# The block in front of a selective scan: input in four parts, one normalisation pipeline for both images, positions added tile by tile

## The chip, the cores and the metric

The kernel runs on one core of a Trainium2 chip. A core has TensorE (PE; PEld is its weight load), VectorE (DVE), ScalarE (ACT), GpSimd (POOL) and SyncE (SP), which here issues the DMAs. The metric is the time of one execution on the device in microseconds; a time "before" or "after" is the median of several.

## The reference

A chain of layers on two images of 256 channels and 48x48 pixels (2304 tokens): a bidirectional selective scan, linear attention, softmax attention, a graph mixture, sigmoid attention and a mixture of experts. Only the very first steps matter here:

```
x:   (2, 256, 2304)                          # channels x tokens, for each image
m, v = mean(x, channels), mean((x - m)**2, channels)
xn   = (x - m) * rsqrt(v + 1e-5) * ln_g + ln_b
xn  += pos_scale * pos                       # pos: (256, 2304), the same for both images
xz   = xn @ in_proj_w.T                      # then convolution, projections, the scan
```

Beside the input the scan needs weights in SBUF, among them the diagonal matrices `ddiag` (the D of each direction on a diagonal), the negated convolution bias `ncb` and `-exp(A_log)` in `alog`.

## The kernel before

Channels lie on the 128 partitions in two halves (`KC` = 2), tokens along the free dimension. `k.X` holds both images, 128 x 2 x 4608 f32. A tile is `T` = 384 tokens, so an image has `NT` = 6 tiles. A block (`nc.Block()`) holds one instruction stream for each engine; all engines meet at its end. `fresh` is a small block after it in which SyncE clears the semaphores that the block used.

The order in front of the scan is written out by hand, block by block:

- `build` sets `k.eps5` in a block (L3796) and calls `load_constants` (L68): SyncE issues the two images (L76) and three 128x128 constants (L80), identity, mean weights and group weights, and waits for all of them.
- `mamba_input` (L247), first block: SyncE issues `pos`, `gb` (gain and bias of the normalisation) and `pscale` on the semaphore `pos_in` (L258 to L260), and ten weight DMAs on `params` (L262 to L270). It waits for none of them, but the block ends when SyncE has issued them.
- `norm_image` (L86), once for each image, a software pipeline over six tiles with three buffers. For one tile: POOL adds the two channel halves (L110); TensorE multiplies by the mean weights (L124), which gives the mean on all partitions in PSUM; DVE subtracts it (L150); ACT squares (L171); POOL adds the halves of the squares (L114); TensorE sums over channels into three columns (L132); ACT takes the root (L178), DVE the reciprocal (L155); TensorE spreads the three columns over all partitions with the identity as moving operand (L139); DVE multiplies (L162). In its stream each engine takes the later steps of earlier tiles behind the first step of a new one, and waits for semaphores in that order.
- `mamba_input`, last block: ACT scales `pos` by `pscale` and adds the bias (L279, two instructions of 2304 columns), then makes `ncb` and `alog` (L282 to L285); DVE multiplies X by the gain and adds `pos` (L295, four of 2304 columns); POOL makes the eight diagonals (L303); SyncE stores the padding (L309).
- `mamba_chunks`: the scan, 20 chunks of 64 steps; its first instruction that reads X is the matmul of L501. Its per-step work: ACT L796, POOL L934, DVE L978 and L989, TensorE L624.

## Time and profile before

| | us |
|---|---|
| median of 3 runs | 5541.01 (5525.89 to 5549.51) |
| the profiled execution | 5545.61 |
| its span, first to last instruction | 5543.8 |
| first matmul of the scan | 97.5 |
| mean granted clock of TensorE | 0.948 of full |

Busy over the span: PE 4723.3 us (85%), DVE 3434.4 (62%), POOL 2317.8 (42%), ACT 2126.5 (38%). The page's 40 slices are 139 us each, so all that the change touches lies in the first of them. There the page can't resolve anything; the views used are the timeline, the waits, the groups of instructions and the table of stretches, all restricted to the first 100 us, and a few rows from later stages that show an operation or a collision that the first 100 us don't have. In the timeline a row is: start in us, time in us, engine, line, operation, written and read tensors, shapes, count (instructions of a kind that follow each other are merged, and the time is that of all of them), and in brackets the engine's idle time before it with what ended it.

### The profile page before, as it was taken

What the parts mean: (1) busy time and instruction counts of PE and PEld (TensorE: products, weight loads), DVE (VectorE), ACT (ScalarE), POOL (GpSimd) and SP (SyncE); (2) the same over time, 40 slices, a digit from 0 to 9 for tenths busy, and PEclk for the clock granted to TensorE, in tenths of its full rate; (3) what the DMA queues carried; (4) which work ended last, traced back from release to release, by engine and by line L of the source; (5) the groups of instructions that cost most, each with busy time, mean ns of one, the idle gap of its engine ahead of it and who ended that gap; (6) DMA issues with size and microseconds to landing.
All of it is one profiled execution on the core that took longest, in us unless ns stands there. A gap on an engine that the chain in (4) does not pass through costs nothing. (4 is left out here: it accounts for less than half of the span.)

```text
span 5543.8 us, 51619 instructions
## 1 busy us (share of the span) xinstructions
PE 4723.3 (85%) x14958; PEld 2624.9 (47%) x14959; DVE 3434.4 (62%) x5148; ACT 2126.5 (38%) x3464; POOL 2317.8 (42%) x2114
## 2 busy tenths in 40 slices
PE   5787788988878888799899899596999899996798
PEld 3333333433323333355455655464555555555576
DVE  2999999999999999679387365264232101003232
ACT  2666666656656666232232222111222222112232
POOL 2888898888889888302111100461000000003111
PEclk7999999999999999999999899798999999995899
DMA  2434443443444443100100001110112000001222
GB/s 85 153 111 145 141 124 123 131 128 117 131 141 130 130 136 109 61 31 6 50 30 15 31 4 42 22 16 15 58 43 89 2 0 2 0 8 36 64 73 93
DMA packets 222219, 391.88 MB, mean 71 GB/s; under 512 B 35986, under 2 KB 205752, under 8 KB 217116
## 3 DMA queue, kind: packets, MB, share of 16 engines
q1 hardware_dynamic: 213852, 383.83, 21.6%
q0 software_dynamic: 8128, 5.27, 0.6%
q8 instruction: 101, 1.65, 0.1%
q14 instruction: 138, 1.13, 0.1%
HBM read 337.13 MB, written 58.23 MB: 71 GB/s over the span
## 5 line engine op out<-in xcount | busy, mean ns | idle before, releaser
L934 POOL TENSOR_TENSOR DBU<-DU,BB 128x461 f32<-128x461 f32 (+1 forms) x1280 | 1372.3, 1087 | 291.7 <-DVE PS L978 279.3
L624 PE MATMUL PS<-G,ident 128*128 128x461 f32 (+1 forms) x2560 | 1138.1, 570 | 385.2 <-DVE G L989 382.5
L978 DVE TENSOR_TENSOR_SCAN PS<-PS,HC,DBU 128x461 f32<-128x461 f32 (+1 forms) x1024 | 1149.5, 1168 | 3.9 <-ACT PS L796 2.5
L796 ACT ACTIVATE PS<-DT,alog 128x461 f32<-128x461 f32 (+1 forms) x1280 | 825.1, 645 | 727.5 <-DVE PS L978 726.7
L624 PEld LDWEIGHTS PS<-G,ident 128*128 128x128 f32 x2560 | 451.9, 190 | 1034.8 <-DVE G L989 822.7
L989 DVE TENSOR_TENSOR G<-PS,CB 128x461 f32<-128x461 f32 (+1 forms) x1280 | 786.6, 625 | 3.4 <-PE PS L624 3.4
L3074 DVE TENSOR_TENSOR X<-X,PS 128x768 f32 x12 | 11.5, 954 | 554.0 <-PE PS L3041 554.0
L3030 PE MATMUL PS<-QT,N 128*128 x864 | 310.1, 486 | 5.5 <-ACTq L3047 5.5
L3041 PE MATMUL PS<-AT,XT 128*128 128x384 f32 x864 | 310.4, 487 | 0.0
L1367 POOL TENSOR_TENSOR X<-X,FF x12 | 42.5, 3542 | 636.7 <-ACT EV L1362 636.7
L978 DVE TENSOR_TENSOR_SCAN PS<-PS,DBU 128x461 f32<-128x461 f32 (+1 forms) x256 | 271.7, 1106 | 57.8 <-POOL DBU L934 55.7
L3105 POOL TENSOR_TENSOR xs<-X 128x384 f32 x12 | 11.7, 989 | 700.6 <-issue 700.6
L1043 PE MATMUL PS<-TT,w_fc 128*128 x768 | 280.9, 494 | 12.2 <-ACTq L1067 12.2
L1053 PE MATMUL PS<-H,w_fc 128*128 128x384 f32 x768 | 275.3, 486 | 0.0
L3063 ACT ACTIVATE AT<-PS 128x384 f32<-128x384 f32 x216 | 105.3, 490 | 416.8 <-PE PS L3030 416.8
L523 PE MATMUL PS<-XI,cdiag 128*128 128x461 f32 (+1 forms) x640 | 260.0, 549 | 0.6 <-ACT XI L680 0.6
L2968 DVE TENSOR_TENSOR Hg<-Hg,GB 128x384 f32<-128x384 f32 x144 | 80.3, 558 | 258.9 <-ACT Hg L2950 248.1
L1081 ACT ACTIVATE H<-PS,b_fc 128x384 f32<-128x384 f32 x192 | 111.0, 580 | 325.7 <-PE PS L1043 325.6
L3030 PEld LDWEIGHTS PS<-QT,N 128*128 128x128 f32 x864 | 164.0, 190 | 119.9 <-issue 5.9
L3041 PEld LDWEIGHTS PS<-AT,XT 128*128 128x128 f32 x864 | 163.7, 190 | 115.5 <-issue 2.6
L2923 PE MATMUL PS<-NN,w1g 128*128 128x384 f32 x576 | 209.4, 492 | 4.4 <-PEq L57 4.4
L2937 PE MATMUL PS<-Hg,w2g 128*128 128x384 f32 x576 | 207.3, 488 | 0.0
(446 smaller groups left out, 7459.0 us busy)
## 6 DMA issues: line engine op xcount, KB each, us to landing
BB<-proj_dram SPq DMA_DIRECT2D x256, 461.0 KB, 4.0
CB<-proj_dram SPq DMA_DIRECT2D x64, 922.0 KB, 6.0
BB<-proj_dram SPq DMA_DIRECT2D x64, 460.0 KB, 4.7
ew<-in_l_w SPq DMA_DIRECT2D x16, 1024.0 KB, 5.7
CB<-proj_dram SPq DMA_DIRECT2D x16, 920.0 KB, 5.9
w_fc<-in_l_w_fc SPq DMA_DIRECT2D x4, 2048.0 KB, 11.7
XI<-xi_dram SPq DMA_DIRECT2D x8, 928.0 KB, 5.0
xi_dram<-XI SPq DMA_DIRECT2D x8, 922.0 KB, 6.5
```

Of the source, the lines that this page charges most:

```text
L523: mm = pe.matmul(PS[:, 2 + j % 2, :wide(h)], w.cdiag[:, j, t, :], XI[:, j, at:at + wide(h)], start=(t == 0), stop=(t == TAP - 1))
L624: pe.matmul(PS[:, j, :wide(g)], k.ident[:], G[:, S % 4, :wide(g)], start=False, stop=(n == DS - 1))\
L796: act.activation(DA(S), DT[:, j, :wide(g)], ACT.Exp, scale=w.alog[:, chunk(g)[1], j, n:n + 1]).then_inc(da_done, 1)
L934: pool.tensor_tensor(DBU[:, S % 4, :wide(g)], DU[:, j, :wide(g)], BB[:, 2 * u + n % 2, :wide(g)], ALU.mult).then_inc(dbu_done, 1)
L978: dve.tensor_tensor_scan(flow(HS(S), g), flow(DA(S), g), flow(DBU[:, S % 4, :wide(g)], g), start, ALU.mult, ALU.add).then_inc(h_done, 1)
L989: dve.tensor_tensor(G[:, S % 4, :wide(g)], HS(S), CB[:, n, :wide(g)], ALU.mult).then_inc(g_done, 1)
L1043: mm = pe.matmul(k.PS[:, s % 3, :T], w1(j, s), src(j, c), start=(j == 0), stop=(j == KC - 1))
L1053: mm = pe.matmul(k.PS[:, 4 + 2 * u + o, :T], w2(m, o), H[:, m, :], start=(m == 0), stop=(m == NM - 1))
L2923: mm = pe.matmul(k.PS[:, s % 3, :T], w1[:, j, s * P:(s + 1) * P], g.NN[:, j, c * T:(c + 1) * T], start=(j == 0), stop=(j == KC - 1))
L2937: mm = pe.matmul(k.PS[:, 4 + 2 * u + o, :T], w2[:, m, o * P:(o + 1) * P], H[:, m, :], start=False, stop=(m == NM - 1))
L3030: mm = pe.matmul(k.PS[:, s % NA, :T], k.N[:, j, s * P:(s + 1) * P], QT[:, j, bass.ds(c * T, T)], start=(j == 0), stop=(j == KC - 1))
L3041: mm = pe.matmul(k.PS[:, 4 + 2 * u + o, :T], XT[:, m, o * P:(o + 1) * P], AT[:, m % NA, :], start=(m == 0), stop=(m == LT - 1))
```

## The change

`load_constants`, `norm_image` and the blocks of `mamba_input` become one block. SyncE issues x in four parts of three tiles, each on its own semaphore, in the order part 0, mean weights, `gb`, `pscale`, part 1, `pos`, part 2, part 3, identity, group weights, then the ten weight DMAs, and then waits for the padding's memset and stores it. All twelve tiles of both images run through one pipeline. The variance is summed by a matmul with the full mean weights, so it stands on all partitions at once (384 columns instead of three, and no spreading matmuls); ACT takes its logarithm, drains, and takes the exponential of -0.5 times that, in place of the root, reciprocal and spread. DVE then multiplies each half of a tile by gain and 1/sigma in one instruction with two SBUF inputs (two instructions of 384 columns), and adds `pos` to the first half; POOL adds `pos` to the second half. ACT scales `pos` in step 3 of the pipeline. The diagonals are made by ACT after the last tile. The block uses 22 semaphores.

```diff
-        load_constants(nc, ctx, k, A)
@@ mamba_input
+    DEEP = 3
+    NV = NB * NT
+    PART = 3
...
+            @block.sync
...
+                load_x(0)
+                sp.dma_start(k.mean_w[:], A["c_mean"]).then_inc(mean_in, 16)
                 sp.dma_start(gb[:], A["l0_ln"]).then_inc(pos_in, 16)
                 sp.dma_start(pscale[:], A["L0_conv_pos_scale"].rearrange("(o n) -> o n", o=1)
                              .broadcast_to([P, 1])).then_inc(pos_in, 16)
+                load_x(1)
+                sp.dma_start(pos[:], A["c_pos"]).then_inc(pos_in, 16)
+                load_x(2)
+                load_x(3)
+                sp.dma_start(k.ident[:], A["c_ident"]).then_inc(const_in, 16)
+                sp.dma_start(k.group_w[:], A["c_group"]).then_inc(const_in, 16)
...
+            @block.gpsimd
...
+                for s in range(NV + 4):
+                    if s < NV:
+                        if s % PART == 0:
+                            pool.wait_ge(x_in[s // PART], 16)
+                        if s >= DEEP:
+                            pool.wait_ge(mean_ready, s - DEEP + 1)
+                        pool.tensor_tensor(xs[:, s % DEEP, :], tile(s)[:, 0, :], tile(s)[:, 1, :], ALU.add)\
+                            .then_inc(x_summed, 1)
+                    if 2 <= s <= NV + 1:
+                        v = s - 2
+                        pool.wait_ge(squared, v + 1)
+                        pool.tensor_tensor(sq[:, v % DEEP, 0, :], sq[:, v % DEEP, 0, :], sq[:, v % DEEP, 1, :], ALU.add)\
+                            .then_inc(sq_summed, 1)
+                    if s >= 4:
+                        v = s - 4
+                        pool.wait_ge(scaled, v + 1)
+                        if v == 0:
+                            pool.wait_ge(pos_done, KC)
+                        n = tile(v)[:, 1, :]
+                        pool.tensor_tensor(n, n, pos[:, 1, v % NT * T:(v % NT + 1) * T], ALU.add)
...
+            @block.tensor
...
+                for s in range(NV + 1):
+                    if s < NV:
+                        pe.wait_ge(x_summed, s + 1)
+                        if s >= DEEP:
+                            pe.wait_ge(centered, s - DEEP + 1)
+                        pe.matmul(k.PS[:, s % DEEP, :T], k.mean_w[:], xs[:, s % DEEP, :], start=True, stop=True)\
+                          .then_inc(mean_ready, 1)
+                    if s >= 1:
+                        v = s - 1
+                        pe.wait_ge(sq_summed, v + 1)
+                        if v >= DEEP:
+                            pe.wait_ge(logged, v - DEEP + 1)
+                        pe.matmul(k.PS[:, DEEP + v % DEEP, :T], k.mean_w[:], sq[:, v % DEEP, 0, :], start=True, stop=True)\
+                          .then_inc(var_ready, 1)
...
             @block.scalar
             def _(act):
+                act.preload_act_table_set("natural_log_exp_and_others")
+                act.wait_ge(eps_set, 1)
+                for s in range(NV + 1):
+                    if s < NV:
+                        act.wait_ge(centered, s + 1)
+                        if s >= DEEP:
+                            act.wait_ge(var_ready, s - DEEP + 1)
+                        act.activation(sq[:, s % DEEP, :, :], tile(s), ACT.Square).then_inc(squared, 1)
+                    if s >= 1:
+                        v = s - 1
+                        act.wait_ge(var_ready, v + 1)
+                        if v >= DEEP:
+                            act.wait_ge(scaled, v - DEEP + 1)
+                        act.activation(rstd[:, v % DEEP, :], k.PS[:, DEEP + v % DEEP, :T], ACT.Ln, bias=k.eps5[:])\
+                           .then_inc(logged, 1)
+                        act.drain()
+                        act.activation(rstd[:, v % DEEP, :], rstd[:, v % DEEP, :], ACT.Exp, scale=-0.5).then_inc(inverted, 1)
+                    if s == 3:
+                        act.wait_ge(pos_in, 48)
+                        for c in range(KC):
+                            act.activation(pos[:, c, :], pos[:, c, :], ACT.Identity, bias=gb[:, c, 1:2], scale=pscale[:])\
+                               .then_inc(pos_done, 1)
                 act.wait_ge(params, 160)
+                act.wait_ge(const_in, 32)
+                for d in range(2):
+                    for j in range(JD):
+                        act.activation(w.ddiag[:, d, j, :], k.ident[:], ACT.Copy, scale=w.vec[:, d, j, 1:2])
...
             @block.vector
             def _(dve):
+                dve.memset(k.eps5[:], 1e-5).then_inc(eps_set, 1)
                 dve.memset(w.neg1[:], -1.0)
...
+                for s in range(NV + 3):
+                    if s < NV:
+                        dve.wait_ge(mean_ready, s + 1)
+                        mean = k.PS[:, s % DEEP, :T].rearrange("p (o t) -> p o t", o=1).broadcast_to([P, KC, T])
+                        dve.tensor_tensor(tile(s), tile(s), mean, ALU.subtract).then_inc(centered, 1)
+                    if 2 <= s <= NV + 1:
+                        v = s - 2
+                        if v == 0:
+                            dve.wait_ge(pos_in, 48)
+                        dve.wait_ge(inverted, v + 1)
+                        for c in range(KC):
+                            n = tile(v)[:, c, :]
+                            op = dve.scalar_tensor_tensor(n, n, gb[:, c, 0:1], rstd[:, v % DEEP, :], ALU.mult, ALU.mult)
+                        op.then_inc(scaled, 1)
+                    if s >= 3:
+                        v = s - 3
+                        if v == 0:
+                            dve.wait_ge(pos_done, KC)
+                        dve.wait_ge(scaled, v + 1)
+                        n = tile(v)[:, 0, :]
+                        dve.tensor_tensor(n, n, pos[:, 0, v % NT * T:(v % NT + 1) * T], ALU.add)
         fresh(nc, used)
```

## Rows read from the trace of the kernel before

**Rows 1.** Table of stretches: start:end, us; busy of PE, PEld, DVE, ACT, POOL; clock; DMA.

```profile
15.30:27.60 12.30, 0.00 (x0) 0.00 (x0) 0.00 (x0) 0.12 (x1) 0.00 (x0) 1.00 0.73 271
52.60:82.10 29.50, 24.15 (x84) 19.33 (x84) 12.52 (x19) 6.20 (x12) 11.67 (x12) 0.51 0.00 1
...
sum 97.50, PE 42.66 PEld 33.13 DVE 35.17 ACT 21.50 POOL 36.97; mean PE 8.53 PEld 6.63 DVE 7.03 ACT 4.30 POOL 7.39
```

**Rows 2.** Waits, 0 to 95 us: who waited for whom, total, times, longest.

```profile
POOL xs L110 <- SPq L102: 32.0, 2, 27.1
```

**Rows 3.** Timeline, the first tiles of image 0.

```profile
27.60 2.88 POOL L110 TENSOR_TENSOR xs<-X 128x384 f32<-128x384 f32 x3 [27.12 <-SPq L102]
...
30.32 0.95 DVE L150 TENSOR_TENSOR X<-X,PS 128x768 f32<-128x768 f32 x1 [29.42 <-PE PS L124]
...
36.25 0.95 DVE L150 TENSOR_TENSOR X<-X,PS 128x768 f32<-128x768 f32 x1 [1.02 <-PE PS L124]
```

**Rows 4.** Timeline, late tiles of image 0.

```profile
43.04 0.94 DVE L150 TENSOR_TENSOR X<-X,PS 128x768 f32<-128x768 f32 x1
...
44.49 0.81 PE L124 MATMUL PS<-xs,mean_w 128*128 128x384 f32 x2
...
45.14 0.92 DVE L162 TENSOR_TENSOR X<-X,PS 128x768 f32<-128x768 f32 x1
45.98 0.95 DVE L150 TENSOR_TENSOR X<-X,PS 128x768 f32<-128x768 f32 x1
```

**Rows 5.** Timeline, TensorE in image 1.

```profile
68.54 1.49 PE L124 MATMUL PS<-xs,mean_w 128*128 128x384 f32 x2
...
72.38 1.49 PE L124 MATMUL PS<-xs,mean_w 128*128 128x384 f32 x2
```

**Rows 6.** Timeline, the last two blocks' borders.

```profile
81.11 0.95 DVE L162 TENSOR_TENSOR X<-X,PS 128x768 f32<-128x768 f32 x1 [0.33 <-PE PS L139]
83.15 0.11 POOL L299 MEMSET pad<- 128x12 f32 x1 [6.34 <-POOLq L57]
...
93.94 2.66 POOL L303 TENSOR_SCALAR ddiag<-ident,vec 128x128 f32<-128x128 f32 x1
97.48 0.11 POOL L876 MEMSET XI<- 128x12 f32 x1 [0.88 <-POOLq L57]
```

**Rows 7.** The line that loads x (L76, issued at 1.17 and 1.7).

```profile
DMA to landing us min/median/max: 8.1/10.6/13.2
```

**Rows 8.** Groups on ScalarE: line, operation, shapes, count; busy us, mean ns; idle.

```profile
L1081 ACT ACTIVATE H<-PS,b_fc 128x384 f32<-128x384 f32 x192 | 111.0, 580 | 325.7 <-PE PS L1043 325.6
...
L279 ACT ACTIVATE pos<-pos,gb,pscale 128x2304 f32<-128x2304 f32 x2 | 4.5, 2299 | 4.6 <-PEq L57 4.6
...
L285 ACT ACTIVATE alog<-alog 128x128 f32<-128x128 f32 x1 | 0.3, 309 | 0.0
```

**Rows 9.** Timeline, diagonals on POOL beside the positions on VectorE.

```profile
84.51 1.18 POOL L303 TENSOR_SCALAR ddiag<-ident,vec 128x128 f32<-128x128 f32 x2
...
85.59 2.62 DVE L295 SCALAR_TENSOR_TENSOR X<-X,gb,pos 128x2304 f32<-128x2304 f32 x1 [2.31 <-ACT pos L279]
85.67 3.01 POOL L303 TENSOR_SCALAR ddiag<-ident,vec 128x128 f32<-128x128 f32 x1
```

**Rows 10.** Timeline, a POOL addition beside VectorE's copies in a later stage.

```profile
2463.39 2.47 POOL L1367 TENSOR_TENSOR X<-X,FF  x1 [154.32 <-ACT EV L1362]
2464.10 6.53 DVE L1832 COPY_PREDICATED V<-MV,V 128x4095 int32<-128x4095 int16 x1
...
2482.26 4.92 DVE L1832 COPY_PREDICATED V<-MV,V 128x4094 int32<-128x4094 int16 x1
...
3054.20 1.80 POOL L1369 TENSOR_TENSOR X<-X,EV 128x768 f32 x1 [0.16 <-issue]
```

**Rows 11.** Table of stretches, the scan and the last stages (columns as in rows 1).

```profile
250.00:355.00 105.00, 83.69 (x200) 35.12 (x200) 105.00 (x161) 64.70 (x97) 89.82 (x85) 1.00 0.43 127
...
4700.00:5543.00 843.00, 744.77 (x2820) 515.28 (x2820) 173.48 (x573) 215.24 (x414) 106.69 (x108) 0.89 0.15 45
```

More of the change, by code:

```diff
@@ L275, in _ @@
             @block.scalar
             def _(act):
-                act.wait_ge(pos_in, 48)
-                for c in range(KC):
-                    act.activation(pos[:, c, :], pos[:, c, :], ACT.Identity, bias=gb[:, c, 1:2], scale=pscale[:])\
-                       .then_inc(pos_done, 1)
+                act.preload_act_table_set("natural_log_exp_and_others")
[20 more added lines that the diff above has]
+                               .then_inc(pos_done, 1)
@@ L3792, in build @@
         k.rd_in = [ctx.enter_context(nc.semaphore(f"rd_in{u}")) for u in range(NU)]
-        with nc.Block() as block:
-            @block.vector
-            def _(dve):
-                dve.memset(k.eps5[:], 1e-5)
-        load_constants(nc, ctx, k, A)
         if start <= 0 <= upto:
```

160 lines of the change are left out of this document (29 added, 131 removed).

## Prediction

> **What bounds the kernel now.** The kernel is a row of stages, one after the other, and the change touches only what lies ahead of the scan. So I first read the table of stretches up to the scan's first matmul, at 97.5 us [rows 1]: loading takes 15.3 us with no engine at work; another 12.3 us pass in which the DMA engines are busy and still no engine; image 0's normalisation takes 25 us, image 1's 29.5 with the gap before it, the positions 15.4. No engine is busy for more than 42.7 of the 97.5 us, so the stretch is bound by its order. The waits [rows 2] name what orders the first part: POOL's additions wait 32.0 us for SyncE's queue, 27.1 of it in one piece. In the code, SyncE issues thirteen DMAs in `mamba_input`'s first block, and every engine waits at the block's end before `norm_image` may start: POOL's first addition comes at 27.60 [rows 3], though x was in by 15.
>
> Then the pace of one tile. In image 0 the chain of subtraction, square, root, reciprocal and product, each engine's step behind another's, closes in 2.94 us (subtractions at 43.04 and 45.98) [rows 4]. In image 1 the granted clock is 0.51, the 1.2 GHz level [rows 1], and TensorE is occupied without a gap: 3.84 us for a tile (68.54 to 72.38) [rows 5]. Between two blocks with the clearing of ten semaphores lie 1.1 us (82.06 to 83.15); from POOL's end to the scan, with six, 0.9 (96.60 to 97.48) [rows 6].
>
> **The change part by part.** The sum is one for the time of the scan's first matmul, now 97.5; what comes after is the same code.
>
> *Start.* x comes in four parts of 1.18 MB. The two images landed 8.1 and 13.2 us after issues at 1.17 and 1.7, at 9.3 and 14.9 [rows 7]; a part is half an image, 2.8 us of that pace, so part 0 lands at 6.5. The mean weights, 64 KB, land some 0.5 us behind it, before POOL's first sum is done (0.96 us [rows 3]). `pos` has part 0, the small ones and part 1 ahead of it: 4.8 MB with itself, as much as was loaded by 15.1, so it lands at about 15.5. Parts 2 and 3 land at 18.5 and 21.5, before POOL needs them; the weights behind them are needed only at the end. Nothing waits any more for SyncE's issuing.
>
> *First three tiles.* The first subtraction came 2.72 us after POOL's first sum and the third 8.65 after [rows 3], which gives 9.2 and 15.2; the fourth, behind a mean that TensorE takes after two variances, at 17.8. The new wait for `pos_in` on VectorE stands before the scaling of tile 0, at 16: `pos` is just in. Behind that wait would be queued all of VectorE's later subtractions.
>
> *The stall.* At step 3 ScalarE, after tile 3's square and tile 2's logarithm and exponential (to 21.0), scales all of `pos`: two activations of 2.30 us [rows 8], to 25.5. Behind them are queued every later square; VectorE's first addition waits for both, and behind that addition the subtraction of tile 4; POOL's first position addition waits too, and behind it the sum of tile 5. So tile 4's subtraction starts, behind tile 0's addition and a POOL addition that holds it off (below), at 26.8, not at 21. Before, the same activations cost 2.31 us of waiting [rows 9].
>
> *Pace of a tile from there.* POOL has three additions of 384 columns. Three of them in a row take 2.88 us [rows 3], so that is the pace by POOL alone. VectorE has the subtraction (0.84 from start to start, 45.14 to 45.98 [rows 4]), two scalings and an addition of 384 columns from SBUF. The trace has no such scaling; the nearest row is the same instruction at 2304 columns, 2.62 us [rows 9], a sixth of which is 0.44; the upper end is the subtraction of 768 from PSUM, 0.84. I take 0.44, the like instruction, and 2.2 us for a tile. ScalarE: square 0.84; a logarithm from PSUM with a bias, 0.58 by the activation of that shape [rows 8]; an exponential, at most the same: 2.0 us, and the drain before the exponential, which no row shows, has 1 us of slack under either pace. TensorE: two matmuls of 384 columns, each 1.49 us at the lower level and 0.81 at the upper [rows 4, 5]: 1.6 to 3.0 us; the short matmuls that made variance and spread go. By busy time alone POOL is the bound, near 2.95.
>
> But VectorE and POOL get into each other's way, and here the trace is plain. POOL's diagonal product, 0.59 us alone (two in 1.18 [rows 9]), took 3.01 when VectorE's scaling with two SBUF inputs had begun 0.08 us before it [rows 9]; the last one took 2.66, ending 0.5 after VectorE's last scaling [rows 6]. The other way round: VectorE's predicated copy of 4095 columns took 6.53 us while a POOL addition of 768 columns was under way, against 4.92 for 4094 columns without one; so it lost 1.61 us to an addition that takes 1.80 alone [rows 10]. In the changed loop VectorE's three new instructions all have two SBUF inputs and POOL is always adding. An addition of 384 columns holds VectorE off for 1.61/2 = 0.80 us; so the shared time of a tile is 3 x 0.80 + 3 x 0.44 = 3.7 us, and 3 x 0.96 + 3 x 0.44 = 4.2 if the whole instruction holds. I take 3.9, between them and nearer the first because that is a measured hold. Ends: 2.95 with no collisions, 4.5 with 0.1 us lost at each of three changes of hand.
> The Trainium skill, "SBUF — State Buffer", section "SBUF: two separate sides", has this as a rule against such a change: a VectorE instruction with two SBUF inputs and a GpSimd instruction lock each other out for the whole instruction. The trace agrees on the lock, but shows 1.61 of 1.80 us held and, in the products, less; by the rule the pace is 4.2 and the sum 2.1 us later, and with no such lock it would be 6.6 us earlier.
>
> *Seven tiles*, from tile 4's to tile 11's subtraction: 7 x 3.9 = 27.3, to 54.1.
>
> *End.* Behind tile 11's subtraction: 0.95, square 0.84, sum 0.96 (and 0.3 waiting), variance 1.7 (a matmul of 1.49 and its end), logarithm and exponential 1.16: 5.9 us. Then ScalarE makes the eight diagonals that POOL made: the nearest rows are its 128-column activations, 0.31 us [rows 8]; 8 x 0.32 = 2.6, and negation, exponential and product for `ncb` and `alog` 0.8. POOL's and VectorE's last additions end about a microsecond earlier. End of ScalarE: 54.1 + 5.9 + 3.4 = 63.4. The block's end and the clearing of semaphores: 1.1 us with ten, 0.9 with six [rows 6], so 0.05 to 0.06 for each, and 0.9 + 16 x 0.06 = 1.85 with 22. The scan starts at 65.2.
>
> *Costs at nothing.* The removed table load of the root lay beside a variance that it had to wait for; the new preload lies in the 6.5 us of loading. The padding's memset and stores go out while tiles are worked on, in front of nothing on SyncE. TensorE idles before the scan in both kernels, so its first matmuls find the clock alike.
>
> *Sum.* 97.5 - 65.2 = 32.3 us less. Against the profiled execution, 5545.6 (span 5543.8 and 1.8 around it): 5513.3. That execution lies 4.6 above the median of 5541.0, and its first 97 us hold no reason for that, so I take the median: 5541.0 - 32.3 = 5508.7.
>
> **Rivals.**
> (a) *No collisions at the pace of the loop.* For it: VectorE's two-input instructions are short and POOL's could fall in between. Against: [rows 9, 10], and POOL would never be idle. Pace 2.95: the end is 7 x 0.95 = 6.6 us earlier; 5502.1.
> (b) *The parts don't come one by one*, or `pos` comes late: part 0 is complete only when parts behind it are, at about 15. Tile 0 then starts 8.7 us later, `pos` is no further wait, and 8.5 us of the gain go; a `pos` landing at 24 instead would cost 6.8. Against: image 0 landed 5.6 us before image 1 though they were issued 0.5 apart [rows 7]. 5541.0 - 23.8 = 5517.2. This is also the case in which the change doesn't do what it says.
> (c) *Slower: the clock in a later stage.* The stretch 4700 to 5543 ran at 0.89 of full clock with TensorE busy 88% of it [rows 11]; the same code took 2.94 us for a tile at the upper and 3.84 at the lower level [rows 4, 5]. If everything after the scan, starting 32 us earlier, meets the clock's changes at other places and this stretch gets 0.82, it is 843 x 0.89/0.82 - 843 = 72 us longer: 5581. It decides from a loss of 60 us on, which is a mean clock of the whole of about 0.937 in place of 0.948. Against: the runs of one kernel would then differ by as much, and they lie within 24 us. The scan itself can't be upset: VectorE is 100% busy in it [rows 11].
> (d) *Part of the gain given back downstream* without a nameable wait, by runs as such: they spread 12 us to either side of the median.
>
> **How the numbers follow.** Main case 0.60, (a) 0.13, (b) 0.18, (c) 0.04, the rest a mixture (0.05). A measurement of this kernel can tell 0.5%, 27.7 us, from no change. The main case lies 4.6 beyond that bound; with its own range, paces 3.5 to 4.5 (2.8 and 4.2 us), and the spread between medians of three, 7 of 10 of it is faster; of (a) 9 of 10, of (b) 3 of 10. That is 0.42 + 0.12 + 0.05 and a little of the rest: 0.60 faster, 0.36 same, 0.04 slower. Range: low is (a) less the run spread, 5502 - 12 = 5490; high is (b) with it, 5517 + 12 = 5529.
>
> **What would show it.** Part 0's first addition at 6.5; a hole between tile 3's and tile 4's subtractions of about 9 us, ended by the activations of `pos`; then subtractions 3.9 us apart, POOL's additions with a mean of 1.2 us or more in place of 0.99, and VectorE's 384-column instructions far above 0.5; ScalarE last, the scan's first matmul at 65. I am wrong if POOL's additions stay at 1.0 us and the pace at 3.0 (a), if POOL starts at 15 (b), if the diagonals or the 22 semaphores take several microseconds, or if the stages behind the scan differ by more than 15 us.

## The result, and the profile after

The changed kernel takes 5501.69 us (median of 20 runs, 5492.73 to 5527.09) against 5535.41 for the kernel before on the same chip (20 runs, 5525.89 to 5558.49). The ratio is 0.9944, 95% interval 0.9930 to 0.9957: faster by some 0.6%, clear of the spread. The medians differ by 33.7 us, where 32.3 were forecast. The profiled execution took 5526.62 us (span 5524.8), and its runs lie in two groups, thirteen up to 5503.9 and seven from 5516.2 on; the profile is of the upper one. So it is read for stages, not for the total.

The scan's own work is the same. These are two of its groups, of the kernel before and then of the changed one (line, engine, operation, names and shape, count; busy us, mean ns; idle before, and releaser):

```profile
L934 POOL TENSOR_TENSOR DBU<-DU,BB 128x461 f32<-128x461 f32 (+1 forms) x1280 | 1372.3, 1087 | 291.7 <-DVE PS L978 279.3
...
L978 DVE TENSOR_TENSOR_SCAN PS<-PS,HC,DBU 128x461 f32<-128x461 f32 (+1 forms) x1024 | 1149.5, 1168 | 3.9 <-ACT PS L796 2.5
```

```profile
L916 POOL TENSOR_TENSOR DBU<-DU,BB 128x461 f32<-128x461 f32 (+1 forms) x1280 | 1371.8, 1086 | 299.2 <-DVE PS L960 286.7
...
L960 DVE TENSOR_TENSOR_SCAN PS<-PS,HC,DBU 128x461 f32<-128x461 f32 (+1 forms) x1024 | 1149.3, 1167 | 5.1 <-ACT PS L778 5.1
```

So the change can act only ahead of the scan. In the two profiled executions what lies behind the start of the scan even took longer, 5458.0 us against 5446.3: 7.6 of the 11.7 us up to the graph mixture, 5.2 in it, and 1.1 less behind it. That part differs by as much between kernels with the same code in it (see e9 and e11).

The timeline of the changed kernel's first 27 us (start, duration, engine, line, operation, operands, count, and the idle time before with its releaser) answers [rows 2, 3]:

```profile
6.51 2.89 POOL L201 TENSOR_TENSOR xs<-X 128x384 f32<-128x384 f32 x3 [5.62 <-DMA X<-in_x]
...
9.30 0.95 DVE L276 TENSOR_TENSOR X<-X,PS 128x768 f32<-128x768 f32 x1 [8.35 <-PE PS L224]
...
15.28 0.95 DVE L276 TENSOR_TENSOR X<-X,PS 128x768 f32<-128x768 f32 x1 [3.75 <-PE PS L224]
...
16.87 1.89 DVE L284 SCALAR_TENSOR_TENSOR X<-X,gb,rstd 128x384 f32<-128x384 f32 x2 [0.64 <-DMA pos<-in_c_pos]
...
19.55 1.13 DVE L284 SCALAR_TENSOR_TENSOR X<-X,gb,rstd 128x384 f32<-128x384 f32 x2
...
21.48 4.49 ACT L256 ACTIVATE pos<-pos,gb,pscale 128x2304 f32<-128x2304 f32 x2
...
26.00 0.56 DVE L292 TENSOR_TENSOR X<-X,pos 128x384 f32<-128x384 f32 x1 [5.32 <-ACT pos L256]
...
26.48 0.95 DVE L276 TENSOR_TENSOR X<-X,PS 128x768 f32<-128x768 f32 x1
```

GpSimd starts at 6.51 in place of 27.60 [rows 3], released by the DMA of part 0 and no longer by SyncE's queue. Then the stall: VectorE sits idle for 5.32 us until ScalarE has scaled all of `pos`, and tile 4's subtraction comes at 26.48.

The loop isn't steady at once. The first tile behind the stall takes 6.18 us, of which VectorE waits 1.34 for the next mean, while TensorE starts again at its lower level (two matmuls in 1.49 us). The second takes 4.32:

```profile
32.66 0.95 DVE L276 TENSOR_TENSOR X<-X,PS 128x768 f32<-128x768 f32 x1 [1.34 <-PE PS L224]
```

Then come four tiles at 3.97 us and a last one at 2.39; the mean of the seven is 4.11. One of the four, from subtraction to subtraction:

```profile
40.94 0.94 DVE L276 TENSOR_TENSOR X<-X,PS 128x768 f32<-128x768 f32 x1
...
41.81 2.71 DVE L284 SCALAR_TENSOR_TENSOR X<-X,gb,rstd 128x384 f32<-128x384 f32 x2
41.84 1.00 POOL L201 TENSOR_TENSOR xs<-X 128x384 f32<-128x384 f32 x1
...
42.84 1.27 POOL L206 TENSOR_TENSOR sq<-sq 128x384 f32<-128x384 f32 x1
...
44.44 0.55 DVE L292 TENSOR_TENSOR X<-X,pos 128x384 f32<-128x384 f32 x1
44.60 1.25 POOL L214 TENSOR_TENSOR X<-X,pos 128x384 f32<-128x384 f32 x1 [0.49 <-DVE X L284]
44.91 0.94 DVE L276 TENSOR_TENSOR X<-X,PS 128x768 f32<-128x768 f32 x1
```

The tile takes 3.97 us, and VectorE has no idle time in it: 0.87 from the subtraction to the scalings, 2.63 to the addition, 0.47 to the next subtraction. VectorE is the bound. Its two scalings, which have two SBUF inputs, take 2.71 us here and took 1.13 at 19.55, where no GpSimd instruction lay beside them. The end of the block:

```profile
61.47 2.43 ACT L262 ACTIVATE ddiag<-ident,vec 128x128 f32<-128x128 f32 x8
...
63.24 1.82 DVE L292 TENSOR_TENSOR X<-X,pos 128x384 f32<-128x384 f32 x2
63.40 1.25 POOL L214 TENSOR_TENSOR X<-X,pos 128x384 f32<-128x384 f32 x1 [1.03 <-DVE X L284]
...
64.23 0.31 ACT L266 ACTIVATE alog<-alog 128x128 f32<-128x128 f32 x1
...
66.77 0.11 POOL L858 MEMSET XI<- 128x12 f32 x1 [2.13 <-POOLq L57]
66.81 1.11 PE L483 MATMUL PS<-X,w_in 128*128 128x461 f32 x1 [6.47 <-PEq L57]
```

The scan's first matmul starts at 66.81, 30.7 us earlier than before (97.5), where 32.3 were forecast.

### The profile page after: what moved, and what is told of

It is laid out like the page before. It is cut to its first block and busy times, and to the rows that moved or that the text cites. A ratio compares the mean times of both kernels' runs of the same rounds, so it can differ in the third digit from the quotient of the medians.

```text
span 5524.8 us, 51351 instructions
## 1 busy us (share of the span) xinstructions
PE 4749.2 (86%) x14838; PEld 2632.5 (48%) x14839; DVE 3446.2 (62%) x5156; ACT 2137.3 (39%) x3482; POOL 2324.0 (42%) x2118
## 5 line engine op out<-in xcount | busy, mean ns | idle before, releaser
L3087 POOL TENSOR_TENSOR xs<-X 128x384 f32 x12 | 11.7, 991 | 700.3 <-issue 398.0
```

## The experiments

All are read first by the start of the scan's first matmul, since what lies behind it varies from run to run by more than most of these edits are worth (last two experiments of this section). The starts vary too: the changed kernel's was 66.8 and, repeated as e9, 67.1; kernels with e1's code ahead of the scan had 60.8 and 60.0, those with e3's 55.1, 56.8 and 56.5. So a difference under 2 us between two starts shows nothing by itself. Times are medians, with the kernel before timed alongside: 5538.82 for e1 to e4, 5577.09 for e5 to e8, 5574.22 for e9 to e12. Only ratios can be compared between these groups.

| kernel | scan starts | time (runs) | ratio to before, 95% interval |
|---|---|---|---|
| before | 97.5 | 5535.41 (20) | 1 |
| changed | 66.8 | 5501.69 (20) | 0.9944 (0.9930 to 0.9957) |
| e1 exponential in PSUM | 60.8 | 5512.46 (12) | 0.9953 (0.9936 to 0.9970) |
| e2 `pos` scaled in pieces | 61.5 | 5497.89 (6) | 0.9929 (0.9905 to 0.9952) |
| e3 both | 55.1 | 5483.47 (6) | 0.9919 (0.9891 to 0.9946) |
| e4 before, issuing moved | 88.0 | 5520.35 (12) | 0.9976 (0.9957 to 0.9995) |
| e5 e1, four matmuls ahead of the graph loop | 60.0 | 5549.3 (10) | 0.9944 (0.9923 to 0.9965) |
| e6 x in two parts | 67.0 | 5566.83 (1) | a single run |
| e7 diagonals on GpSimd | 70.9 | 5575.78 (1) | a single run |
| e8 e3, four matmuls ahead of the graph loop | 56.8 | 5535.07 (7) | 0.9924 (0.9897 to 0.9950) |
| e9 changed, again | 67.1 | 5544.71 (12) | 0.9947 (0.9925 to 0.9969) |
| e10 changed, old root chain | 68.9 | 5533.44 (6) | 0.9927 (0.9895 to 0.9958) |
| e11 e3 again | 56.5 | 5532.13 (6) | 0.9917 (0.9885 to 0.9950) |
| e12 positions behind the loop | 60.0 | 5526.62 (1) | a single run |

**e1: is the pace the collision of VectorE with GpSimd?** The exponential goes to PSUM, so that the scalings read one operand from SBUF and one from PSUM, with the one wait that this needs.

```diff
-act.activation(rstd[:, v % DEEP, :], rstd[:, v % DEEP, :], ACT.Exp, scale=-0.5).then_inc(inverted, 1)
+act.activation(k.PS[:, DEEP + v % DEEP, :T], rstd[:, v % DEEP, :], ACT.Exp, scale=-0.5).then_inc(inverted, 1)
...
-    pe.wait_ge(logged, v - DEEP + 1)
+    pe.wait_ge(scaled, v - DEEP + 1)
...
-    op = dve.scalar_tensor_tensor(n, n, gb[:, c, 0:1], rstd[:, v % DEEP, :], ALU.mult, ALU.mult)
+    op = dve.scalar_tensor_tensor(n, n, gb[:, c, 0:1], k.PS[:, DEEP + v % DEEP, :T], ALU.mult, ALU.mult)
```

> The changed kernel, with the exponential written to the tile's variance bank in PSUM, so that VectorE's two scalings have one SBUF input each instead of two. Lock theory (VectorE and POOL hold each other off only where VectorE has two SBUF inputs): the scalings fall from a mean of 1.10 us to about 0.6, POOL's additions from 1.17 to about 1.03, the pace of a tile from 3.97 to about 3.1 (POOL's own 2.86 and a part of the one addition that still collides), and the scan starts at 61 instead of 66.8. Rival (the pace is that of the chain from subtraction to scaling, or of TensorE at the lower clock level, and the long times only reflect it): pace 3.9 as before, scan at 66 to 67.

The group of the scalings, of the changed kernel and then of e1 (columns as in the first fence):

```profile
L284 DVE SCALAR_TENSOR_TENSOR X<-X,gb,rstd 128x384 f32<-128x384 f32 x24 | 25.4, 1099 | 0.7 <-DMA pos<-in_c_pos 0.6
```

```profile
L284 DVE SCALAR_TENSOR_TENSOR X<-X,gb,PS 128x384 f32<-128x384 f32 x24 | 13.6, 606 | 3.3 <-DMA pos<-in_c_pos 2.0 <-ACT PS L252 1.3
```

One scaling costs 1.10 us on average with two SBUF inputs and 0.61 with one, beside the same GpSimd. The pace falls to 3.20 and the scan starts 6.0 us earlier. VectorE still has no idle time in a tile, so it is the missing hold and not a waiting engine that made the pace, which rules out the rival. What is left of the collisions sits in the positions' addition, which still has two SBUF inputs. Timeline of e1:

```profile
41.58 0.94 DVE L276 TENSOR_TENSOR X<-X,PS 128x768 f32<-128x768 f32 x1
42.45 1.13 DVE L284 SCALAR_TENSOR_TENSOR X<-X,gb,PS 128x384 f32<-128x384 f32 x2
42.48 1.01 POOL L214 TENSOR_TENSOR X<-X,pos 128x384 f32<-128x384 f32 x1
...
43.49 1.35 DVE L292 TENSOR_TENSOR X<-X,pos 128x384 f32<-128x384 f32 x1
```

**e2: what does scaling `pos` in two long activations cost?** ScalarE scales it tile by tile, in steps 2 to 7.

```diff
-if s == 3:
-    act.wait_ge(pos_in, 48)
+if 2 <= s < NT + 2:
+    if s == 2:
+        act.wait_ge(pos_in, 48)
     for c in range(KC):
-        act.activation(pos[:, c, :], pos[:, c, :], ACT.Identity, bias=gb[:, c, 1:2], scale=pscale[:])\
+        part = pos[:, c, (s - 2) * T:(s - 1) * T]
+        act.activation(part, part, ACT.Identity, bias=gb[:, c, 1:2], scale=pscale[:])\
            .then_inc(pos_done, 1)
...
-if v == 0:
-    dve.wait_ge(pos_done, KC)
+if v < NT:
+    dve.wait_ge(pos_done, KC * (v + 1))
```

> The changed kernel, with the scaling of pos on ScalarE in twelve pieces of 384 columns, two in each of the pipeline's steps 2 to 7, instead of two of 2304 in step 3. Stall theory: the hole of 5.3 us on VectorE before its first addition goes, ScalarE's load of 3 us for a tile stays below the pace of 3.97, tile 4's subtraction comes at 22 instead of 26.5 and the scan starts at 62. Rival (the stall only let the other engines catch up, or ScalarE's extra 1 us for a tile lies in the chain): the pace of tiles 0 to 5 grows by 0.7 and the scan starts at 66.

```profile
22.11 1.35 DVE L294 TENSOR_TENSOR X<-X,pos 128x384 f32<-128x384 f32 x1
...
23.38 0.94 DVE L278 TENSOR_TENSOR X<-X,PS 128x768 f32<-128x768 f32 x1
```

In e2's timeline tile 4's subtraction comes at 23.38, where it came at 26.48, the pace stays at 3.9 to 4.2, and the scan starts 5.3 us earlier. The stall of the forecast is there, and is worth that: 3.1 us at tile 4, and 2.2 in the seven tiles up to tile 11's subtraction (26.5 us in place of 28.8), since the slow first tile behind the stall is gone too.

**e3: both.** The two diffs together.

> Both edits together: exponential to PSUM and pos scaled in twelve pieces. If the two costs are independent, the gains add: 5.6 and 4.8 us, scan at 56.5, total some 10 us below the changed kernel. Rival: with the collisions gone ScalarE (3.1 us for a tile in six tiles) or TensorE at the lower level (3.0) become the pace and only 7 of the 10 us are left, scan at 59 to 60.

The scan starts at 55.05: 11.8 us earlier than in the changed kernel, where the two gains add up to 11.3; with the other two starts of this code it is 10.0 and 10.3. So the gains add, as far as the starts can tell. The rival, 59 to 60, is out. With e11, the same kernel, it has the lowest ratio of all that were run several times, though the intervals overlap.

**e4: how much of the gain is SyncE's issuing alone?** The kernel before, with the thirteen issues moved out of their own block into that of image 0's normalisation.

```diff
-        with nc.Block() as block:
-            @block.sync
-            def _(sp):
-                sp.dma_start(pos[:], A["c_pos"]).then_inc(pos_in, 16)
+        def issue(sp):
+            sp.dma_start(pos[:], A["c_pos"]).then_inc(pos_in, 16)
...
-            norm_image(nc, k, b, k.eps5, k.X[:, :, b * L:(b + 1) * L])
+            norm_image(nc, k, b, k.eps5, k.X[:, :, b * L:(b + 1) * L], issue if b == 0 else None)
```

> The kernel before, with one thing changed: SyncE issues pos and the ten weight DMAs inside the block of image 0's normalisation instead of in a block ahead of it. This measures how much of the change is the loading order alone. If POOL's first addition waited for nothing but SyncE's issuing, it comes at 16.3 instead of 27.6 and the scan starts at 86.2: 11.3 us less in all, a third of the whole change. Rival (the normalisation would have to wait for something else, or the issuing costs it as much inside the block): the scan still starts at 95 or later.

```profile
16.52 2.89 POOL L115 TENSOR_TENSOR xs<-X 128x384 f32<-128x384 f32 x3 [16.04 <-POOLq L57]
```

GpSimd starts 11.1 us earlier, but image 0's loop now runs at TensorE's lower level (3.84 us a tile, as image 1's [rows 5]), and 9.5 us reach the scan. So 9.5 of the 30.7 are had by moving a block's border; 21.2 are for the rest of the change, 10.0 of them already there when GpSimd starts (6.51 against 16.52), because neither all of x nor the other constants need be in by then.

**e6: are four parts worth it?** x comes in one part for each image, and `pos` between them.

```diff
-    PART = 3
+    PART = 6
...
-                load_x(1)
                 sp.dma_start(pos[:], A["c_pos"]).then_inc(pos_in, 16)
-                load_x(2)
-                load_x(3)
+                load_x(1)
```

> The changed kernel with x loaded in two parts, one for each image, in the order image 0, mean weights, gb, pscale, pos, image 1. What the four parts are worth: POOL starts when image 0 has landed, 2.8 us later than now, at 9.3; the wait for pos (0.6 us now) goes, so the scan starts 2.2 to 2.8 us later, at 69.0 to 69.6. Rival (the stall at the scaling of pos takes up the delay): the scan starts at 67.

```profile
9.14 2.89 POOL L199 TENSOR_TENSOR xs<-X 128x384 f32<-128x384 f32 x3 [8.26 <-DMA X<-in_x]
...
21.66 4.49 ACT L254 ACTIVATE pos<-pos,gb,pscale 128x2304 f32<-128x2304 f32 x2
26.18 0.56 DVE L290 TENSOR_TENSOR X<-X,pos 128x384 f32<-128x384 f32 x1 [5.55 <-ACT pos L254]
...
26.66 0.95 DVE L274 TENSOR_TENSOR X<-X,PS 128x768 f32<-128x768 f32 x1
```

The start is 2.6 us later, yet the scaling of `pos` begins at 21.66 in place of 21.48, and the scan starts 0.2 us later, which is less than the changed kernel's own two starts differ. In the changed kernel the 2.6 us are lost again in its wait for `pos` and at the lower clock level (two matmuls for a mean take 1.49 us there, 0.81 here). The expectation failed and its rival, 67, holds: dividing x in four buys nothing that can be seen as long as the loop waits for the scaling of `pos`.

**e7: are the diagonals well placed on ScalarE?**

```diff
-                for d in range(2):
-                    for j in range(JD):
-                        act.activation(w.ddiag[:, d, j, :], k.ident[:], ACT.Copy, scale=w.vec[:, d, j, 1:2])
...
+                pool.wait_ge(params, 160)
+                pool.wait_ge(const_in, 32)
+                for d in range(2):
+                    for j in range(JD):
+                        pool.tensor_scalar(w.ddiag[:, d, j, :], k.ident[:], w.vec[:, d, j, 1:2], None, ALU.mult)
```

> The changed kernel with the eight diagonals made by POOL behind its last position addition, as the kernel before had them on POOL, instead of by ScalarE. If their move to ScalarE took them off the path that ends last, the scan now starts 8 x 0.59 = 4.7 us later than 66.8, at 71.5. Rival (the end is set by something else, ScalarE's or VectorE's last instructions or the clearing of semaphores): 67 to 68.

```profile
64.17 4.98 POOL L219 TENSOR_SCALAR ddiag<-ident,vec 128x128 f32<-128x128 f32 x8
...
70.94 1.11 PE L484 MATMUL PS<-X,w_in 128*128 128x461 f32 x1 [10.87 <-PEq L57]
```

The scan starts 4.1 us later, with the diagonals behind GpSimd's last addition. On ScalarE (2.43 us) they end before VectorE does (ScalarE at 64.54, VectorE at 65.06), and cost nothing.

**e10: what is the swap of root and reciprocal for logarithm and exponential worth?** The changed block with the old chain in it, the identity loaded ahead for it, and the scalings reading the spread from PSUM.

```diff
-act.activation(rstd[:, v % DEEP, :], k.PS[:, DEEP + v % DEEP, :T], ACT.Ln, bias=k.eps5[:])
-act.drain()
-act.activation(rstd[:, v % DEEP, :], rstd[:, v % DEEP, :], ACT.Exp, scale=-0.5).then_inc(inverted, 1)
+act.activation(rstd[:, v % DEEP, :], k.PS[:, DEEP + v % DEEP, 0:T // P], ACT.Sqrt, bias=k.eps5[:])
...
+dve.reciprocal(rstd[:, v % DEEP, :], rstd[:, v % DEEP, :]).then_inc(inverted, 1)
...
+mm = pe.matmul(k.PS[:, DEEP + v % DEEP, P + t * P:2 * P + t * P],
+               rstd[:, v % DEEP, t:t + 1].broadcast_to([P, P]), k.ident[:], start=True, stop=True)
...
-op = dve.scalar_tensor_tensor(n, n, gb[:, c, 0:1], rstd[:, v % DEEP, :], ALU.mult, ALU.mult)
+op = dve.scalar_tensor_tensor(n, n, gb[:, c, 0:1], k.PS[:, DEEP + v % DEEP, P:P + T], ALU.mult, ALU.mult)
```

> The changed block with the old chain in it: root, reciprocal and the spreading of three columns by TensorE, instead of logarithm and exponential; the scalings then read the spread from PSUM. Theory: the swap takes four short TensorE instructions and a VectorE one out of each tile, but makes the two scalings read both inputs from SBUF beside GpSimd, and the one about pays for the other. With the old chain the scalings take 0.61 us, as in the run with the exponential in PSUM, and TensorE sets the pace: 3.84 us a tile at the lower clock level, as for image 1 of the kernel before, so that the scan's first matmul starts at 65.5 to 68 and the time is within 3 us of the changed kernel's. Rival: TensorE or the longer chain of small steps limits it more, pace 4.5 us or over, scan at 71 or later. Other rival: the clock rises with more work on TensorE (2.95 us a tile), scan at 60 to 61.

```profile
38.38 0.95 DVE L283 TENSOR_TENSOR X<-X,PS 128x768 f32<-128x768 f32 x1
...
39.03 1.63 PE L239 MATMUL PS<-ident,rstd 128*128 128x128 f32 x6
...
40.45 1.49 PE L224 MATMUL PS<-xs,mean_w 128*128 128x384 f32 x2
...
42.22 0.95 DVE L283 TENSOR_TENSOR X<-X,PS 128x768 f32<-128x768 f32 x1
```

3.84 us a tile, as expected, and 3.60 once TensorE has risen to its upper level at 46 us. (The levels are read from how long matmuls take. The clock column of the table of stretches isn't reliable so early in an execution: for e10 it says 1.00 from 36 to 42, while a mean took 1.49 us.) The scan starts at 68.93, 0.9 above the expected span. So the swap is worth 2.1 us of the 30.7 in the start of the scan, hardly more than starts vary, and the times cannot tell the two kernels apart. It relieves TensorE and charges VectorE almost as much, through the very operand that e1 moves. Against e1, which also reads 1/sigma from PSUM, the old chain starts the scan 8.1 us later: the swap pays once that operand is out of SBUF.

**e12: what is adding the positions tile by tile worth?** Each tile is scaled by one instruction over both halves, and the positions are added behind the loop, as in the kernel before [rows 9].

```diff
-for c in range(KC):
-    n = tile(v)[:, c, :]
-    op = dve.scalar_tensor_tensor(n, n, gb[:, c, 0:1], rstd[:, v % DEEP, :], ALU.mult, ALU.mult)
-op.then_inc(scaled, 1)
+root = rstd[:, v % DEEP, :].rearrange("p (o t) -> p o t", o=1).broadcast_to([P, KC, T])
+dve.tensor_tensor(tile(v), tile(v), root, ALU.mult).then_inc(scaled, 1)
...
-dve.tensor_tensor(n, n, pos[:, 0, v % NT * T:(v % NT + 1) * T], ALU.add)
...
-pool.tensor_tensor(n, n, pos[:, 1, v % NT * T:(v % NT + 1) * T], ALU.add)
...
+for c in range(KC):
+    dve.wait_ge(pos_done, c + 1)
+    for b in range(NB):
+        n = k.X[:, c, b * L:(b + 1) * L]
+        dve.scalar_tensor_tensor(n, n, gb[:, c, 0:1], pos[:, c, :], ALU.mult, ALU.add)
```

> The changed block with the positions added behind the pipeline again, by four whole-image VectorE instructions as in the kernel before (2.63 us each, 10.5 in all), and each tile scaled by one instruction over both halves; GpSimd adds no positions. Theory: the adds tile by tile cost about 0.7 us a tile of pace (3.97 against some 3.2) and save 10.5 less 1.3 at the end, so that without them the pipeline ends 5 to 6 us earlier, the block ends 3 to 5 us later, and the scan starts at 70 to 72. Rival: the pace doesn't fall (TensorE at the lower level or the lock on the scaling holds it at 3.9), scan at 75 or later. Other rival: the adds in the loop cost as much as they save, scan at 67.

```profile
19.73 0.94 DVE L269 TENSOR_TENSOR X<-X,PS 128x768 f32<-128x768 f32 x1
...
39.32 0.95 DVE L269 TENSOR_TENSOR X<-X,PS 128x768 f32<-128x768 f32 x1 [0.83 <-PE PS L217]
...
41.23 1.00 POOL L206 TENSOR_TENSOR sq<-sq 128x384 f32<-128x384 f32 x1 [0.93 <-ACT sq L236]
...
41.95 0.95 DVE L269 TENSOR_TENSOR X<-X,PS 128x768 f32<-128x768 f32 x1 [0.81 <-PE PS L217]
...
48.06 10.21 DVE L281 SCALAR_TENSOR_TENSOR X<-X,gb,pos 128x2304 f32<-128x2304 f32 x4
...
60.02 8.40 PE L472 MATMUL PS<-X,w_in 128*128 128x461 f32 x16 [14.21 <-PEq L57]
```

The expectation had the wrong sign: the scan starts at 60.02, 6.8 us earlier than with the positions tile by tile, and none of the three cases named was near. Tile 4's subtraction comes at 19.73 in place of 26.48, since nothing in the loop waits for ScalarE's scaling ahead of it: 6.75 us. From tile 4's to tile 11's subtraction it takes 22.2 us in place of 28.8, though ScalarE's 4.49 us now fall into it (7.13 us between the subtractions at 22.31 and 29.44): 6.5 us. What stands behind tile 11's subtraction takes 18.1 us in place of 11.6: 6.5 us back. The last was expected as 9.2, the two gains together as 5 to 6 where they are 13.3: the wait was left out, and the pace expected, 3.2, is the mean over the seven tiles (3.17), but has to be set against the changed kernel's mean of 4.11 and not against 3.97. The steady pace is 2.6 to 2.9. It is a round of subtraction, square, GpSimd's sum and two matmuls, which serves two tiles in 5.3 us; no single engine is full in it, as in image 0 of the kernel before [rows 4]. Where GpSimd comes second it is held off here too, longer than in the changed kernel, because the one scaling over both halves is longer (0.94 us):

```profile
34.94 1.77 POOL L201 TENSOR_TENSOR xs<-X 128x384 f32<-128x384 f32 x1
```

The edit changes three things, the place of the additions, the form of the scaling and the wait in the loop, and most of what it gains is the wait's: beside e2, which takes away the stall and keeps the positions in the loop (61.5), e12 is only 1.5 us earlier, and e3 and its repeats (55.1 to 56.8) are ahead of it. Its one run had a span of 5524.9.

**e5, e8: the clock in the graph mixture.** Behind the scan nothing differs between these kernels but the moment at which it starts; yet 10 of e1's 12 runs lay between 5510 and 5524, and two between 5490 and 5495. The table of stretches of the graph mixture's normalisation (busy of PE, PEld, DVE, ACT, POOL; granted clock; DMA) of the changed kernel, and then of e3, is plain about what happens in it:

```profile
3440.00:3455.00 15.00, 15.00 (x60) 12.88 (x59) 6.00 (x9) 1.99 (x4) 5.71 (x6) 0.50 0.36 151
3455.00:3470.00 15.00, 15.00 (x64) 13.79 (x64) 4.94 (x9) 2.99 (x6) 5.08 (x6) 0.50 0.00 0
```

```profile
3425.00:3440.00 15.00, 15.00 (x121) 13.85 (x121) 8.61 (x13) 4.93 (x10) 7.82 (x9) 1.00 0.06 19
```

In both TensorE is busy all the time; in one it does 60 matmuls in 15 us at 0.50 of full clock, in the other 121 at 1.00. The loop's twelve first additions take 47.7 us in the one (3428.5 to 3476.2) and 32.5 in the other (3408.4 to 3440.9): 15.2 us, all of it TensorE's own busy time (44.98 against 29.74 us). e5 and e8 put four matmuls of 384 columns ahead of that loop, to have it begin at the upper level.

```diff
+for _ in range(4):
+    pe.matmul(k.PS[:, 5, :T], k.ident[:], k.X[:, 0, 0:T], start=True, stop=True)
 for s in range(NG + 3):
```

> e1 with four extra matmuls of 384 columns (identity times X, into a bank that is not in use yet) at the start of TensorE's stream in the normalisation ahead of the graph mixture, 3419 us into the run. Ten of e1's twelve runs lay at 5510 to 5524 and two at 5490 to 5495; its profiled one, of the upper group, shows that loop at the lower clock level throughout (47.7 us for twelve tiles), while kernels of the lower group show it at the upper level from its fourth tile (32.5 us). Clock theory: the two groups are that loop with the clock risen or not; with TensorE busy at its start the clock rises, the loop takes 33 to 37 us, and the runs gather at 5492 to 5500 with a mean granted clock of 0.948. Rival (the clock in the loop comes out as it does whatever runs ahead of it, or the groups come from another stage): the extra work costs 4 us and the runs stay in two groups, most of them at 5514 to 5527.

> e3 (exponential to PSUM and pos in twelve pieces) with the four extra matmuls of e5. Five of e3's six runs lay at 5479 to 5490 and one at 5511. Clock theory: all runs at 5479 to 5493, none above 5505. Rival (the extra matmuls don't change the clock's course): some runs above 5505, and the others 4 us above e3's, at 5483 to 5494.

The theory fell. In e5 the four matmuls themselves ran at the lower level (0.53 of full clock from 3417.8 to 3421.0); the clock was at 0.92 from 3420 to 3425, at 0.76 in the next 5 us and at 0.50 from 3430 on, with TensorE busy without a gap. The loop took 49.0 us, as did e8's, whose clock went to 0.50 at 3425. The ratios to before didn't improve either (e5 0.9944 after 0.9953 for e1, e8 0.9924 after 0.9919 for e3). Four matmuls ahead of the loop didn't keep the clock up in it.

**e9, e11: the changed kernel and e3 side by side.**

> The changed kernel itself, unchanged, on the same chip as the three that follow. The theory on the spread (the graph mixture's normalisation either stays at the clock's lower level, loop of 47.7 to 49.0 us, or rises in it, 32.5 us, and the whole kernel is then some 15 to 25 us apart) expects times in two clusters again, and a profile whose time belongs to the cluster that its own loop says. A rival, that the change made the lower level there more frequent than it was in the kernel before (in whose profile that loop took 32.2 us), expects the kernel before on this chip to lie in one cluster only.

> Exponential in PSUM and the position scaling in twelve pieces, again, beside the changed kernel on one chip. Its block ended 11.8 us earlier than the changed kernel's in the first look (scan at 55.05 against 66.8). Theory: the gain reaches the end of the kernel unchanged, so that this kernel is 10 to 13 us below the changed one when members of the same cluster are compared, ratio of the two times 0.998. Rival: what is saved in front of the scan is partly given back where the graph mixture's clock decides, and the medians differ by under 5 us or by over 20.

e9's runs don't fall into two clusters: they spread over 40 us, 5525.62 to 5565.41, and the kernel before over 49 on this chip, 5553.44 to 5602.21. In e9's profile the loop took the short way, 32.5 us, and its time, 5539.06, is the third lowest of twelve. So the theory doesn't hold here, and the rival isn't supported: the kernel before spreads as widely. The loop's clock is one cause among others. Whether the change made the lower level more frequent is open: the loop was short in both profiles with the old code ahead of the scan (before, e4) and long in six of twelve with the new. The profiles do show where the rest is. From the loop's first addition to the first matmul of the experts behind it:

| | before | changed | e1 | e2 | e3 | e4 | e5 | e6 | e7 | e8 | e9 | e10 | e11 | e12 |
|---|---|---|---|---|---|---|---|---|---|---|---|---|---|---|
| that stage, us | 471 | 476 | 469 | 452 | 444 | 445 | 504 | 521 | 523 | 507 | 490 | 493 | 490 | 479 |
| the loop in it, us | 32.2 | 47.7 | 47.7 | 32.5 | 32.5 | 32.6 | 49.0 | 47.7 | 47.7 | 49.0 | 32.5 | 32.4 | 32.6 | 32.4 |

Behind it every one of them needs 1620 to 1629 us, and from the scan's first matmul to it 3353 to 3364. That stage alone has 32 us of spread from before to e4 and 44 from e5 to e12, of which the loop makes some 15. Within it a stretch of 50 us with a clock near 0.6 can stand where another run has 1.00. e9 and e3, each about 150 to 200 us into the stage:

```profile
3576.80:3626.80 50.00, 29.00 (x131) 16.71 (x129) 18.34 (x33) 5.01 (x7) 31.36 (x29) 0.62 0.08 13
```

```profile
3558.40:3608.40 50.00, 49.34 (x327) 35.61 (x326) 38.22 (x70) 11.36 (x17) 40.55 (x32) 1.00 0.13 22
```

Whether the low clock makes that part late, or a late part the low clock, no run here tells.

e11 has its scan at 56.5, 10.6 us ahead of e9's, and its median is 12.6 below e9's (5532.13 against 5544.71, a quotient of 0.9977): what the theory expected, but with spreads of 23 and 40 us the medians could have said otherwise. The start of the scan, 10 to 12 us earlier in every pairing, is the firmer reading, and the time is in keeping with it.

## Why the prediction was right, point by point

- **Start and first tiles: right.** Part 0 at 6.5 (6.51), subtractions at 9.2 and 15.2 (9.30, 15.28). `pos` came later than the 15.5 forecast: it released VectorE at 16.87, where it was to be "just in" at 16, and tile 3's subtraction came at 18.69 and not at 17.8. Rival (b) is out: the parts do come one by one. But what this is worth was never asked, only what its failure would cost; e6 shows 0.2 us, within the spread, because the scaling of `pos` stands behind it either way.
- **Stall: right.** Tile 4's subtraction was forecast for 26.8 and came at 26.48, released as named. Two misses cancel in it: ScalarE was through at 25.97 and not at 25.5, and the hold of VectorE's first addition didn't come (0.56 us, GpSimd's began 0.11 later). e2 prices the removal of the stall at 5.3 us.
- **Pace: right in its result, partly by luck.** 3.9 forecast, 3.97 measured in the steady tiles. The hold taken from [rows 10], 0.80 us for an addition of 384 columns, is confirmed: two scalings take 2.71 us beside GpSimd and 1.13 without, (2.71 - 1.13) / 2 = 0.79, and e1's addition takes 1.35 in place of 0.55. But the sum said three holds and three instructions at 0.44 us, 3.7, with the subtraction beside them. It is two holds, 1.58, and VectorE's own 2.39: subtraction 0.87, scalings 1.05, addition 0.47. GpSimd's third addition falls beside the subtraction, which has only one SBUF input, and holds nothing. A scaling of 384 columns costs 0.57 alone (1.13 for two), some 30% more than the 0.44 got from the long instruction of [rows 9]. Counting a third hold (0.80) in place of the subtraction (0.87) did almost no harm, because the two happen to be alike; and going from the sum's 3.7 to 3.9 for a hold that might be longer made good the instructions that were priced too low.
- **The rule of the Trainium skill** ("SBUF — State Buffer", section "SBUF: two separate sides"), that the two lock each other out for the whole instruction: the lock is there, for 0.79 of the 1.00 us that an addition of GpSimd takes. With the 1.61 of 1.80 us of [rows 10], some 0.2 us of the recorded time are free of it at either length, so going by these two, a forecast for another length would take the recorded time less 0.2 (an estimate) rather than a share of it.
- **Seven tiles and end: 1.1 and 0.5 us short.** Tile 11's subtraction at 55.24, forecast 54.1: the seven tiles took 28.8 us and not 27.3, because the steady pace was taken to begin at once, and the tile behind the stall took 6.18. Then 9.8 us, forecast 9.3, to the last engine's end. Here "ScalarE last" failed. ScalarE's own 9.3 us are right, diagonals included (8 in 2.43 us, forecast 2.6): it ended at 64.54. But VectorE, put a microsecond ahead of it, ended at 65.06, since the last tile's scaling (1.72 us) and then the additions of tiles 10 and 11 are queued behind one another on VectorE.
- **Semaphores: right.** From VectorE's end to the first matmul 1.75 us, 1.85 forecast; e3 and e12, with the same 22, have 1.74 and 1.75.
- **Sum:** 1.14 + 0.52 - 0.10 = 1.56, the difference between 66.81 and 63.4 + 1.85 = 65.25. The forecast of 5508.7 us is for a kernel before of 5541.0; the 20 runs put that at 5535.4. Less 32.3 that would be 5503.1, and 5501.7 was measured. That the time fell by 33.7 us, more than the 30.7 by which the scan starts earlier, isn't explained by the change; both lie within the interval of the ratio (24 to 39 us).
- **The signs that it named:** GpSimd's additions have a mean of 1.17 us (1.2 or more forecast), the hole between tile 3's and tile 4's subtractions is 7.8 us (9), the scalings' mean is 1.10 (far above 0.5). The stages behind the scan differ by 11.7 us between the two profiles, under the 15 named, but later executions show that this sign means little: the graph mixture alone varies by more.
- **Rival (a), no collisions,** was worth 6.6 in the sum; e1 takes away the scalings' share and gives 6.0. **Rival (d), something given back behind the scan,** shows in the two profiles (11.7 us longer) and not in the medians of 20 runs.
- **Rival (c), the clock in a later stage,** named the wrong place and had an argument that was too lax. The stretch that it names didn't move: from the experts to the end 1620.3 us against 1621.4. But in the graph mixture the clock does what the rival feared, 15 us in one loop, within a stage that varies by 30 to 45. "The runs lie within 24 us" came from three runs; twenty of the same kernel spread 33, nineteen in the last round 49. It didn't decide here: the spreads of before and after are alike (33 and 34 us in twenty runs each).
- **What the prediction left out** is that one part could have been a loss inside a gain. The positions' 15.4 us behind the loop were counted as removed and their additions as part of the pace; the kernel with the new loop and the old positions was not costed, and it would have started the scan 6.8 us earlier (e12), mainly because nothing in its loop waits for the scaling of `pos`.

## What to carry over

Cost every part of a bundle against the bundle without it, not only against the kernel before: of the 30.7 us here, 9.5 come from one block border (e4), the swap of functions brings about 2 (8 with its result in PSUM), the division of the loads nothing that could be seen, and the positions in the loop, with the stall that they bring, cost 6.8. In a pipeline in which GpSimd is hardly ever idle, give VectorE's instructions one operand from PSUM: it was worth 6.0 us in twelve tiles for three edited lines. And an in-order engine that must prepare something long should do it in pieces of the loop's own size (e2, 5.3 us), or nothing in the loop should wait for it (e12). Positions behind the loop together with the exponential in PSUM weren't tried.

## What the runs showed of the hardware that was not expected

- TensorE, busy without a gap in one and the same loop, stays at 0.50 of full clock for 30 us in one execution (changed kernel, 3440 to 3470) and runs at 1.00 in another (e3, 3425 to 3440). Four matmuls ahead of it ran at the lower level themselves (0.53, e5); the clock rose behind them (0.92) and was back at 0.50 within 10 us.
- The lock works both ways, and for a little less than the recorded instruction. A GpSimd addition holds VectorE off for 0.79 us of its 1.00, in scalings (2.71 against 1.13 for two) and additions (1.35 against 0.55) alike, and for 1.61 of 1.80 at twice the length. GpSimd's additions of 1.00 us take 1.25 to 1.31 behind a VectorE instruction of 0.57 us and 1.71 to 1.77 behind one of 0.94 (e12). In the kernel before, an addition of 1.80 us that began at 2466.01, during VectorE's copy of [rows 10], took 6.25 and ended 1.63 behind the copy.
- A subtraction with one input from PSUM took 0.94 us beside a GpSimd addition (44.91) and 0.95 alone: no hold.
- In loops with a shorter round TensorE was at its upper level more often: at 2.63 us a tile its two matmuls for a mean took 0.81 us (e12), at 3.97 they took 1.49 (changed kernel). It isn't shown which is the cause. In neither loop does TensorE set the pace by itself.
